# Another order of the same steps at both ends of a fused attention and FP4 feed-forward kernel

## The reference

```
y = layernorm(x)
y = layernorm(y + attention(y, y, y, causal)) * g1 + beta1
y = layernorm(y + attention(y, ctx, ctx)) * g2 + beta2
y = layernorm(y + relu(y @ w1 + b1) @ w2 + b2) * g3 + beta3     # w1: 256 x 1024
x = x + y
q(t): scale = max|t| over 16 / 6; t / scale is rounded to the grid 0, .5, 1, 1.5, 2, 3, 4, 6, then times scale
n = layernorm(x)
h = silu(q(n) @ q(w_gate).T) * (q(n) @ q(w_up).T)               # 704 wide
x = x + q(h) @ q(w_down).T
```

## Time and profile before

| what | value |
|---|---|
| runs | 595.23, 597.59, 596.07 us; median 596.07 |
| profiled execution | 594.27 us, span 592.4 us |
| granted clock, mean over the span | 0.994 |
| instructions | 12500 |
| DMA | 19.31 MB, 18743 packets |

### The profile page before, as it was taken

One profiled execution on the slowest core, in us unless ns is written; L12 is line 12 of the kernel. 1 busy time (PEld: TensorE's weight loads), 2 busy tenths in 40 slices (PEclk: granted clock), 3 DMA queues, 4 the chain that ended last, 5 costly groups with the idle time before them and its releaser, 6 DMA issues.

```text
span 592.4 us, 12500 instructions
## 1 busy us (share of the span) xinstructions
PE 555.3 (94%) x4042; PEld 529.0 (89%) x4042; DVE 477.2 (81%) x1222; ACT 372.0 (63%) x778; POOL 387.8 (65%) x463
## 2 busy tenths in 40 slices
PE   4687899999999999999999999999999999899885
PEld 2576799999999999999999999999999999889885
DVE  4989888787878878797878878797878878787776
ACT  3766575867667665867667665867667764746331
POOL 3658776675867766675867766675867666666532
PEclk9998999999999999999999999999999999999989
DMA  7701010010101010010101010010201010000000
GB/s 225 249 2 37 0 46 1 3 53 1 63 3 55 2 44 19 2 51 0 62 0 53 0 44 18 5 48 0 62 2 37 2 36 1 19 2 19 0 11 28
DMA packets 18743, 19.31 MB, mean 33 GB/s; under 512 B 1536, under 2 KB 18192, under 8 KB 18704
## 3 DMA queue, kind: packets, MB, share of 16 engines
q1 hardware_dynamic: 18704, 18.82, 10.3%
HBM read 14.62 MB, written 4.19 MB: 32 GB/s over the span
## 4 chain that ended last, share of the span: by engine, by line
PE 59%; DVE 14%; issue 6%; ACT 5%; POOL 5%; DVEq 0%; ACTq 0%; POOLq 0%
PE O L1180 5%; PE TR L1032 4%; PE R L1198 4%; PE R L1200 4%; PE R L1199 4%; PE R L1032 4%; PE O L1226 3%; PE O L1228 3%; PE O L1227 3%; PE R L1127 3%; PE R L1129 3%; PE R L1128 3%; PE O L1251 3%; PE O L1252 2%; PE O L1253 2%
## 5 line engine op out<-in xcount | busy, mean ns | idle before, releaser
L466 POOL TENSOR_TENSOR rs<-mv,neg_half 128x1 f32<-128x1 f32 (+1 forms) x112 | 70.4, 630 | 32.3 <-DVE mv L1604 32.3
L1198 PE MATMUL R<-y2T_hi,w_hi 128*128 128x256 f32 x256 | 77.1, 301 | 3.4 <-DVE y2T_lo L1732 1.7
L1127 PE MATMUL R<-gu_hi,xqT_hi 128*128 128x352 f32 x240 | 78.9, 329 | 0.4 <-DVE xqT_lo L1678 0.4
L1129 PE MATMUL R<-gu_hi,xqT_lo 128*128 128x352 f32 x240 | 77.3, 322 | 0.0
L1128 PE MATMUL R<-gu_lo,xqT_hi 128*128 128x352 f32 x240 | 77.2, 322 | 0.0
L1251 PE MATMUL O<-w_hi,hT_hi 128*128 128x256 f32 x256 | 73.7, 288 | 1.1 <-POOL hT_lo L501 1.1
L1200 PE MATMUL R<-y2T_hi,w_lo 128*128 128x256 f32 x256 | 72.6, 284 | 0.0
L1199 PE MATMUL R<-y2T_lo,w_hi 128*128 128x256 f32 x256 | 72.6, 284 | 0.0
L1253 PE MATMUL O<-w_hi,hT_lo 128*128 128x256 f32 x256 | 71.8, 280 | 0.0
L1252 PE MATMUL O<-w_lo,hT_hi 128*128 128x256 f32 x256 | 71.7, 280 | 0.0
L591 POOL TENSOR_TENSOR xq<-xa,x_div 128x256 f32<-128x256 f32 x32 | 26.4, 824 | 63.4 <-DVE xa L1673 63.4
(11 more groups left out here) (194 smaller groups left out, 1858.6 us busy)
## 6 DMA issues: line engine op xcount, KB each, us to landing
x_in<-in_x SPq DMA_DIRECT2D x16, 256.0 KB, 2.8
x_res<-in_x SPq DMA_DIRECT2D x16, 256.0 KB, 2.8
out<-x SPq DMA_DIRECT2D x32, 128.0 KB, 1.9
ctx_rows<-in_ctx SPq DMA_DIRECT2D x16, 64.0 KB, 2.5
hT<-in_L_xattn_w SPq DMA_DIRECT2D x1, 1024.0 KB, 8.7
hh<-in_L_xattn_w SPq DMA_DIRECT2D x1, 768.0 KB, 7.6
wd_raw<-in_L_ffn_w_down SPq DMA_DIRECT2D x1, 704.0 KB, 8.9
w_raw<-in_L_ffn_w_gate SPq DMA_DIRECT2D x1, 640.0 KB, 4.6
```

Source lines behind the costliest of these rows:

```text
L466: pool.tensor_tensor(rs[i][:, t0:t0 + len(ts)], mv[i][:, t0:t0 + len(ts), 1], neg_half[:, 0:len(ts)], ALU.pow).then_inc(ln_rstd[i], 1)
L1127: mm(o, xh, gu_hi[:, c, m, cols], start=(c == 0), stop=False)
L1129: last = mm(o, xl, gu_hi[:, c, m, cols], start=False, stop=(c == KC - 1))
L1198: mm(o, w1_hi[:, c, cols], y2T_hi[:, c, :], start=(c == 0), stop=False)
```

## The change

Nothing is added or removed. In head() and tail() of all four computing engines the same steps are put in another order, except that relu and relu_upper of the chunk pairs 2 and 3 are each called once for both. The steps of a slot in between stay.

On PE, in the head: the third chunk of ff1 comes before turn_y0(1, 0), the fourth behind cross(1, 0); the turn of weight group 2 comes between chunk pairs of ff1; keep_busy moves from before the values of (1, 0) to right before turn_z2; fold_b1(2) moves up. In the tail: down of (g, 0) moves before the first gate product, split_turn before the third, and the second run of down of (g, 1) before last_turn. On the other engines the order is as the diff has it (lines that stay are left out).

```diff
--- before.py
+++ after.py
@@ -615,8 +615,8 @@
+                unscale_h(b, g, 1)
-                unscale_h(b, g, 1)
@@ -630,7 +630,6 @@
-                after_shift(0, 0, 1, 0)
@@ -639,34 +638,35 @@
+                shift2_row_set()
+                masks(0, 1)
-                masks(0, 1)
+                y_rows(1, 0, False, 0)
-                shift2_row_set()
-                y_rows(1, 0, False, 0)
-                y_rows(1, 0, False, 1)
-                after_shift(0, 0, 2, 0)
+                y_rows(1, 0, True, 0)
+                after_shift(0, 0, 1, 0)
+                y_rows(1, 0, False, 1)
+                y_rows(1, 0, True, 1)
-                y_rows(1, 0, True, 0)
-                y_rows(1, 0, True, 1)
+                masks(1, 0)
-                masks(1, 0)
+                context_values(1)
-                context_values(1)
-                after_shift(2, 1, 0, A)
+                after_shift(2, 1, 0, A)
+                after_shift(0, 0, 2, 0)
@@ -946,18 +946,18 @@
+                abs_x(b, g, 0)
-                abs_x(b, g, 0)
+                split_upper(b, g)
+                last_silu(b, h, 1, 1)
-                split_upper(b, g)
-                last_silu(b, h, 1, 1)
@@ -969,55 +969,53 @@
+                norm_x(0, 1)
-                norm_x(0, 1)
+                w1_upper(0)
-                w1_upper(0)
+                context_upper(0)
+                affine_turned(0, 1, A, n1_turned, y1T, g1_col, beta1_col, y1T_set)
-                affine_turned(0, 1, A, n1_turned, y1T, g1_col, beta1_col, y1T_set)
+                w1_upper(1)
-                w1_upper(1)
-                context_upper(0)
+                exp_rest(0, 1)
-                exp_rest(0, 1)
+                norm(1, 1, 0, A, 0, 1, z1[:, 0, :], z1[:, 0, :])
-                norm(1, 1, 0, A, 0, 1, z1[:, 0, :], z1[:, 0, :])
-                norm(1, 1, 0, A, 1, 1, z1[:, 1, :], z1[:, 1, :])
+                w_abs(2)
-                w_abs(2)
+                norm(1, 1, 0, A, 1, 1, z1[:, 1, :], z1[:, 1, :])
+                affine_turned(1, 0, A, n1_turned, y1T, g1_col, beta1_col, y1T_set)
-                affine_turned(1, 0, A, n1_turned, y1T, g1_col, beta1_col, y1T_set)
+                exp_scores(1, 0)
-                exp_scores(1, 0)
+                exp_cross(1, 0)
-                exp_cross(1, 0)
-                relu(1, 0, (2,))
-                relu_upper(1, 0, (2,))
-                relu(1, 0, (3,))
-                relu_upper(1, 0, (3,))
+                relu(1, 0, (2, 3))
+                relu_upper(1, 0, (2, 3))
+                w_abs(4)
+                w_upper(act, 3)
+                w_abs(5)
-                w_upper(act, 3)
-                w_abs(4)
-                w_abs(5)
@@ -1435,21 +1433,21 @@
+                down_run(b, g, 0, 0, FIRST_RUN)
-                down_run(b, g, 0, 0, FIRST_RUN)
+                down_run(b, g, 0, FIRST_RUN, IC)
-                down_run(b, g, 0, FIRST_RUN, IC)
+                split_turn(b, g)
-                split_turn(b, g)
+                down_run(b, g, 1, FIRST_RUN, IC)
-                down_run(b, g, 1, FIRST_RUN, IC)
@@ -1459,44 +1457,44 @@
+                turn_context(0)
-                turn_context(0)
+                turn_z1(0, 1)
+                scores_rest(0, 1, (0,))
+                w_turn(0, 0, 0, 0)
-                turn_z1(0, 1)
-                w_turn(0, 0, 0, 0)
-                scores_rest(0, 1, (0,))
+                scores_rest(0, 1, (1,))
-                scores_rest(0, 1, (1,))
+                fold_b1(2)
+                values(1, 0, 0)
+                values(1, 0, 1)
+                w_turn(1, 0, 2, 1)
-                values(1, 0, 0)
-                values(1, 0, 1)
-                w_turn(1, 0, 2, 1)
-                fold_b1(2)
-                ff1(1, 0, (0, 1))
+                ff1(1, 0, (0, 1, 2))
-                ff1(1, 0, (2,))
-                ff1(1, 0, (3,))
+                ff1(1, 0, (3,))
+                w_turn(2, FC // 2, 0, 0)
+                ff1(1, 0, (6,))
-                ff1(1, 0, (6, 7))
+                ff1(1, 0, (7,))
-                w_turn(2, FC // 2, 0, 0)
@@ -1988,57 +1986,57 @@
+                h_scale(b, g, 1)
+                h_reciprocal(b, g, 1)
-                h_scale(b, g, 1)
-                h_reciprocal(b, g, 1)
+                hT_lower(b, g, 0)
+                z3_stats(b, g, 1)
-                z3_stats(b, g, 1)
+                scaled_sum(b, g, 1)
-                scaled_sum(b, g, 1)
+                last_shift(b, g, 1)
-                hT_lower(b, g, 0)
-                last_shift(b, g, 1)
+                rows_drop(b, g, 1)
-                last_max(b, h, 0, 0)
-                rows_drop(b, g, 1)
+                last_max(b, h, 0, 0)
-                down_add(b, g, 0)
+                last_product(b, h, 1, 1)
+                rows_lift(b, h, 0)
+                last_max(b, h, 1, 1)
-                rows_lift(b, h, 0)
-                last_product(b, h, 1, 1)
-                last_max(b, h, 1, 1)
+                down_add(b, g, 0)
+                part_lift(1)
-                down_add(b, g, 1)
-                part_lift(1)
+                down_add(b, g, 1)
@@ -2073,40 +2071,40 @@
-                shift(0, 0, 1, 0, (0, 1))
+                shift(0, 0, 1, 0, (0, 1))
+                w1_lower(0)
-                w1_lower(0)
-                w_lower(0)
+                ctx_lower(0)
-                ctx_lower(0)
+                cross_reciprocal(0, 1)
-                cross_reciprocal(0, 1)
+                self_part(1, 0, 0)
-                self_part(1, 0, 0)
+                w_lower(0)
+                shift(1, 1, 0, A, (0, 1))
-                shift(1, 1, 0, A, (0, 1))
-                shift(0, 0, 2, 0, (0, 1))
+                shift(0, 0, 2, 0, (0, 1))
+                w_lower(1)
-                w_lower(1)
@@ -2114,27 +2112,27 @@
-                h_lower(1, 0, (1,))
+                h_lower(1, 0, (1,))
+                cross_sum(1, 0)
-                cross_sum(1, 0)
+                w_amax(4)
-                w_amax(4)
+                w_reciprocal(2)
-                w_reciprocal(2)
-                x_stats(1, 1)
+                x_stats(1, 1)
+                w_lift(4)
+                w_drop(4)
-                w_lift(4)
-                w_drop(4)
```

## The result

The changed kernel takes 602.70 us (median of 5 runs, 602.06 to 604.75), the kernel before 597.59 (5 runs, 595.23 to 598.50): ratio 1.0113, 95% interval 1.0089 to 1.0137. It is slower by more than the 0.5% that this can tell, and lies above the range. Its profiled execution took 602.90 us, span 600.4, 8.0 us over that of before. The same event in both traces comes 4.4 us later at ff1, 4.5 at the end of the head, 6.4 at the end of the middle, and 8.0 at the end.

The account below looks back on a forecast made before the run. PE, busy 94%, paces the middle, so only head and tail can change: head -0.2 us plus tail +0.7 gives +0.5 on the median of 596.07, so 596.6 us, range 593.4 to 599.0.

Parts of the forecast that it names:

- The rest of the scores ahead of the cross transposes: Head: cross(0,1) some 0.6 us later on PE, but DVE read its result only after two weight splits, one now gone.
- z1's turn held by w_abs(2): Head, ff1: y0T's copy behind w_abs(2) puts z1's turn at 43.1 us, not 40.18; PE idles some 3.2 us.
- ff2 has no wait inside: Head's end: the 1.08 us wait inside ff2 goes, since GpSimd then has its part ready.
- the half-rate case: Head: with the clock at half rate, ff2 starts at 55.2 us, against 54.1 at full rate and 53.01 before.
- The idle 3.4 us before down(g,1) and the half rate behind it: Tail: PE waits about 3.4 us for split_lower; half rate then makes the end 0.4 to 1.0 us later.
- The lift ahead of the shift: Head's end: w_lift(4), w_drop(4) ahead of the shift; third reciprocal to second ff_sum takes 4.6 us, not 5.6.
- The head up to ff1: To 37 us: no work added, first z2 at its old time within 0.3 us, ff1 0.6 us late at 37.2.
- in a place where PE has the turn to wait for in any case: Head: the four fillers, 0.25 us each, right ahead of z2's turn, lie in a wait of PE.
- behind w_lift(0) and self_part: Head: norm_x(0,1) now comes behind these two; first z2 still at its old time within 0.3 us.
- The clock: Head, ff1: half rate again after idle PE, over z1's turn, scores and cross; ff1's second half up to 1.3 us later.
- The tail: From 557 us: the new order costs +0.7 us, or gains 0.35 us without half rate.
- I expect full rate here: Tail: down(g,0)'s 18 matmuls fill the thin stretch, so the first 24 gate matmuls run at full clock, ending at 569.0 us.

Follow-up runs that it names:

- e15: Kernel before, with scores_rest(0,1,1) ahead of turn_cross on PE and exp_rest ahead of cp_upper on ACT: ratio 1.0004 to the kernel before.
- e12: Kernel before with the new tail, split_lower(g) ahead of last_product(1,0), and w_lift(4), w_drop(4) ahead of shift(3,1,0): reciprocal to second ff_sum 5.61 us, 6.30 before.
- e18: Kernel before with only w_lift(4) and w_drop(4) ahead of shift(3,1,0) on DVE: ff1 to second ff_sum 26.10 us.
- e9: Changed kernel with the old order on all four engines up to cross_max(0,1): runs 602.79 to 606.53 us but for one; ff1 at 39.22 us.
- e14: Kernel before with shift(0,0,1) behind w_lift(0) and self_part(0,1,0), and y0T's copy behind w1_upper(0): ratio 1.0041 to the kernel before, 2.4 us.
- e17: Kernel before with late shift(0,0,1), late y0T copy, and fillers and w_turn(1) ahead of turn_z2: ratio 1.0054 to the kernel before, 3.2 us.
- e13: Kernel before with the four fillers and w_turn(1) moved ahead of turn_z2 on PE: ratio 1.0009 to the kernel before over 10 runs.
- e2: Changed kernel with the four PE fillers back ahead of values(1,0): ratio 0.8 us lower than the changed kernel's, inside the intervals; ff1 at 39.53 us.
- e1: Changed kernel with the head of all four engines as before, so only the tail is new: ratio 1.0037 to the kernel before, 2.2 us.
- e4: Changed kernel with fillers back ahead of values(1,0), and shift(0,0,1) and y0T's copy early again: ff1 at 39.98 us.
- e6: Changed kernel with DVE's head as before: ratio above the changed kernel's, inside the intervals; ff1 to second ff_sum 29.28 us.
- e7: Changed kernel with PE's head as before: equals the changed kernel by the ratio; ff1 to second ff_sum 28.13 us.
- e3: Changed kernel with shift(0,0,1) ahead of w_lift(0) and y0T's copy ahead of w1_upper(0) again: ff1 at 41.22 us.

## Why the prediction was wrong

**Right.** The rest of the scores ahead of the cross transposes changes nothing (e15). z1's turn held by w_abs(2) (4.6 us behind ff1; 5.9 expected, as GpSimd took 1.51 us for the rows and not 2.81, so that PE idled 1.80, not 3.2, and kept its clock; w_lower(1) now stands ahead of w2_lower on DVE, so that w2_lower did not run beside those rows "as before"). ff2 has no wait inside. That it came 18.1 us behind ff1, against 16.9 to 18.0 summed, is luck: 18.0 was the half-rate case, and here the clock stayed at 1.00 until 60.1 us and z1's turn came earlier than summed, but PE waited 3.51 us for hT_lo. The idle 3.4 us before down(g,1) and the half rate behind it (3.35 us, 585.7 to 589.1). The lift ahead of the shift, in part: 0.7 us of the 1.0 counted in e12 and e18, of which 0.3 last into the next slot, and 0.2 in the changed kernel (6.10 us from the reciprocal to the second ff_sum, which waited 0.36 for PE's ff2).

**The step that failed** is "The head up to ff1": it has the first z2 "at its old time within 0.3 us" and ff1 0.6 us late. z2 was normed 3.1 us late and turned 5.0 us late, and ff1 was 4.4 us late. Two sentences of it were wrong, each for a reason that the trace of before could have shown. First, the fillers "in a place where PE has the turn to wait for in any case": before, z2 was normed at 33.6 (32.52 and 1.09) and PE ended the values at 33.67. PE had nothing to wait for, so 0.57 and 1.0 us of work stood in front of the turn; DVE, busy with statistics to 35.81, hid half (0.8 us are left at ff1 in e9). Second, norm_x(0,1) "behind w_lift(0) and self_part": this put the shift behind a wait of DVE for w_abs(0), and from there the delay went over y0T, the scores and the cross products to the sum, 0.9 to 1.4 us late (e14 and the changed kernel); by itself it costs 2.4 us, 0.9 to 3.9 by the interval. I had looked at what each step needs and not at who then is late. Both together cost 3.2 of the head's 4.5 us (e17); the rest was not found.

**The clock** was weighed at 43 us and in the tail, not here. In the changed kernel's profile it fell from 19.1 to 22.6 and from 29.4 to 36.2 us, and all five of its runs have the same mean, 0.982. It made 2.4 us of the order's 0.8 at ff1 (e13 against e9). The starts of the fillers are 0.43 us apart in e2 and 0.23 before, the two levels of 1.2 and 2.4 GHz. But an idle PE was not what stood right ahead of the fall at 29.4: it was busy 2.69 of the 3 us before it, the 16 one-column matmuls of fold_b1 among it. Before, it was busy 2.65 of the same 3 us, and the clock stayed. What in the head decides whether the clock falls stays open: it fell in old heads too, only not in each run.

**The tail**: 1.7 us where +0.7 was summed (e1: 2.2 by the ratio; over the profiles of the old tail and of the whole new one the fillers are 34.4 to 36.4 us from the end with the old tail, median 35.3 of 7, and 35.4 to 37.9 with the new, median 36.9 of 11). The mechanism of the second half was right, the wait for split_lower and its size. The term that was mis-sized is the stretch from the first gate product to down(g,1): 13.4 us were summed, 14.97 measured; it started 0.6 us earlier than summed, and the difference is the 1.0 us that was missing. "I expect full rate here" is one part of it: the gate products ran at half rate from 572.1 to 575.5 us, as before. But that part is only 0.5 us, since most of the slower matmuls lie in the wait for the second turn of xq. In the profiles where they ran at full rate (e2, e4, e6, e7, e9) the stretch still took 14.46 to 14.49. The other 1.1 us are the order's: the second turn of xq comes 5.6 us behind the first gate product and not 5.0, as PE waits 0.8 for GpSimd, and the second 24 gate products end 5.5 us behind that turn and not 5.1. Of down(g,0) only the first run, 12 matmuls and not 18, moved behind the fillers; the other 6 stand behind the first gate products, inside that wait.

**The base.** The forecast stands on a median of 596.07 for before; beside the result it was 597.59, which is up to 1.5 of the 6.1 us between forecast and result. The 1.8 us between the profiled run and that median, which I took over without a reason, are the size of five long slots (5 x 0.39).

## What to carry over

A step is covered only if the queue behind it has slack: take the time at which its engine arrives and the time at which the operand is ready, from the same trace, before calling a place free. Price a delay in a sparse head twice, at full and at half rate, since the low clock then lies on whatever is late. To find which move of a re-laid order costs, make it alone in the kernel before; taking it back inside the new order also measures the mismatch of the engines, and which steps then run side by side (e3). A gain has to be followed for one slot more before it is counted (e12, e18).
